# Kernel tables of a state-space mixer fetched as triangles, two channel groups interleaved

## What is computed

```
x, z = split(W_in @ hidden)
x = silu(conv4(x) + conv_b)
k = 2 * real(sum over n of Ct[h,n] * exp(dtA[h,n] * t)),  t = 0..511
y = causal_convolution(x, k) + x * D
y = y * silu(z);  out = W_out @ y
x1 = layernorm(hidden + out)
result = layernorm(x1 + expert_of(x1))      # 8 experts 128 -> 512 -> 128, the best one per token
```

## Time and profile before

| what | us |
|---|---|
| median of 3 executions | 283.48 (282.91 to 284.63) |
| the profiled execution, its own time | 282.02 |
| its span in the profile | 280.3 |
| projection until PE's last x product | 0 to 81.6 |
| group loop, PE | 83.8 to 131.6 |
| rest | 131.6 to 280.3 |

### The profile page before, as it was taken

How to read it: one execution, slowest core, us unless ns; L and a number is a source line. 1 busy time by engine, 2 the same in 40 slices (tenths; PEclk the granted TensorE clock), 3 DMA queues, 4 the chain that set the end, 5 groups by cost and what they waited for, 6 DMA issues and landing times.

```text
span 280.3 us, 8864 instructions
## 1 busy us (share of the span) xinstructions
PE 246.5 (88%) x2759; PEld 219.7 (78%) x2760; DVE 180.0 (64%) x585; ACT 177.2 (63%) x496; POOL 116.2 (41%) x175
## 2 busy tenths in 40 slices
PE   7999999999989799998988797375999999997970
PEld 4688888888878678776988696265989999897970
DVE  2689995997237688885445357720787666564772
ACT  4959999645997476764547061504667777675650
POOL 5000000400027576772254655573046565654555
PEclk9999999999999999999999959866899999999997
DMA  6619877549607999994933102713657666676500
GB/s 213 255 60 372 289 293 281 202 146 288 204 9 224 265 286 312 324 306 104 363 124 114 51 29 61 215 59 99 176 165 197 194 181 186 190 203 184 169 32 5
DMA packets 53627, 52.07 MB, mean 186 GB/s; under 512 B 4543, under 2 KB 42945, under 8 KB 53218
## 3 DMA queue, kind: packets, MB, share of 16 engines
q1 hardware_dynamic: 50866, 46.66, 54.8%
q0 software_dynamic: 2304, 4.34, 4.4%
q10 hardware_dynamic: 432, 0.79, 0.9%
HBM read 38.17 MB, written 14.05 MB: 186 GB/s over the span
## 4 chain that ended last, share of the span: by engine, by line
PE 72%; issue 8%; DVE 5%; another core or an unknown queue 4%; ACT 4%; DMA 4%; POOL 1%; SPq 1%; ACTq 0%; DVEq 0%; POOLq 0%
PE banks L1306 20%; PE banks L1510 9%; PE banks L1500 9%; PE banks L1384 6%; PE banks L1289 5%; PE banks L1455 4%; PE banks L1398 4%; PE banks L1394 3%; PE banks L1371 3%; PE banks L1446 2%; PE banks L1432 2%; ACT RE L770 2%; PE banks L1331 1%; DMA out<-X 1%
## 5 line engine op out<-in xcount | busy, mean ns | idle before, releaser
L807 ACT ACTIVATE Z<-banks,BR 128x128 f32<-128x128 f32 x156 | 44.7, 371 | 26.5 <-PE banks L1500 18.2
L1306 PE MATMUL banks<-Wx,XT 128*128 128x256 f32 x256 | 60.4, 382 | 0.0
L1306 PEld LDWEIGHTS banks<-Wx,XT 128*128 128x128 f32 x256 | 49.2, 192 | 7.0 <-issue 0.2
L576 POOL DMA_INDIRECT out<-X x39 | 38.4, 985 | 30.1 <-DVE X L1247 14.7
L1500 PE MATMUL banks<-Z 128*128 128x128 f32 x312 | 44.7, 289 | 6.0 <-ACT Z L796 4.2
L516 POOL TENSOR_TENSOR Wx<-BR,RE 128x384 f32 (+1 forms) x32 | 31.8, 1015 | 40.6 <-PE banks L1306 27.1
L1500 PEld LDWEIGHTS banks<-Z 128*128 128x128 f32 x312 | 40.8, 204 | 7.0 <-ACT Z L796 4.4
L1510 PE MATMUL banks<-BR,Z 128*128 x312 | 42.1, 279 | 0.7 <-DVE X L1230 0.7
L568 POOL DMA_INDIRECT dispatched_rows<-TR,CR x32 | 30.7, 960 | 25.9 <-DVE CR L1155 16.7
L1510 PEld LDWEIGHTS banks<-BR,Z 128*128 128x128 f32 x312 | 38.8, 196 | 1.1 <-issue 1.1
L1230 DVE TENSOR_TENSOR X<-banks,X 128x128 f32<-128x128 f32 x39 | 11.3, 289 | 22.5 <-PE banks L1510 15.8
(11 more groups left out here) (220 smaller groups left out, 455.5 us busy)
## 6 DMA issues: line engine op xcount, KB each, us to landing
TR<-kernel_rows SPq DMA_DIRECT2D x32, 512.0 KB, 6.3
Z<-w SPq DMA_DIRECT2D x39, 256.0 KB
dispatched_rows<-TR SPq DMA_DIRECT2D x3, 2310.0 KB, 9.0
X<-dispatched_rows SPq DMA_DIRECT2D x39, 66.0 KB
XT<-hidden_t SPq DMA_DIRECT2D x10, 256.0 KB, 4.2
RE<-decay_and_turns SPq DMA_DIRECT2D x2, 1024.0 KB, 5.2
BR<-w SPq DMA_DIRECT2D x1, 2048.0 KB, 8.1
dispatched_rows<-TR SPq DMA_DIRECT2D x1, 1848.0 KB, 7.9
```

The lines of the kernel that those rows point to most:

```text
L576: pool.indirect_dma_start(out_rows, bass.IndirectOffsetOnAxis(XS[:, n % ROWS_RING, TOKEN_COL:TOKEN_COL + 1].bitcast(U32), 0), F[:, slot, : ...
L807: last = nc.scalar.activation(HT[:, j, c * P:c * P + P], bank[UP_BANKS[j]][:, c * P:c * P + P], ACT.Relu, bias=B1[:, bass.ds(experts[j] * ...
L1306: last = mm(bank[X_BANKS[k]][:, j * CHAN:(j + 1) * CHAN], XT[:, slot, at:at + CHUNK], Wx[:, tap, :], start=(tap == 0), stop=(tap == TAPS - 1))
```

## The change

A pair of groups now shares one table tile. Two groups' kernel rows are interleaved sample by sample (`Kx` and `kernel_rows` have the pair index innermost), a ring slot holds a pair (4 slots of twice the size), and two transfers fill it: partitions 0 to 63 get 256 interleaved numbers per channel (1024 bytes in a run), partitions 64 to 127 get only the first 128 (512 bytes in a run). The rest of the lower half, the corner, is zeroed once per slot by Pool. PE reads the moving operand with a step of two elements and waits once per pair. The selectors, the order of groups in the kernel-row sums and the layout of `d_skip` follow. Besides, SP loads `cw_row` first, then `prm`, `row_params`, `cbias`; ACT runs a first Exp on one number, then the exponentials of `prm`, then those of `row_params`, and DVE follows that order.

```diff
-T_SLOTS = 8
+T_SLOTS = 4
+HALF = P // 2
...
-    kext = nc.dram_tensor("kernel_rows", [CHAN, KROW], F32).ap()
+    kext = nc.dram_tensor("kernel_rows", [P, KROW, 2], F32).ap()
-    toeplitz = bass.AP(kext.tensor, 0, [[1, P], [KROW, CHAN], [1, CHUNK]])
+    upper_rows = bass.AP(kext.tensor, 0, [[2, HALF], [KROW * 2, P], [1, 2 * CHUNK]])
+    lower_rows = bass.AP(kext.tensor, 2 * HALF, [[2, HALF], [KROW * 2, P], [1, 2 * HALF]])
...
-        TR = sb("TR", [P, T_SLOTS * GH * CHUNK])
+        TR = sb("TR", [P, T_SLOTS * GH * 2 * CHUNK])
...
+        Tpairs = TR[:, :].rearrange("p (s h u j) -> p s h u j", s=T_SLOTS, h=GH, j=2)
...
-            sp.dma_start(row_params, state_rows).then_inc(s_rparams, 16)
-            sp.dma_start(prm[:, :, :], states).then_inc(s_params, 16)
             sp.dma_start(cw_row[:, :], conv_w.rearrange("t c -> (t c)").unsqueeze(0)).then_inc(s_cw, 16)
+            sp.dma_start(prm[:, :, :], states).then_inc(s_params, 16)
+            sp.dma_start(row_params, state_rows).then_inc(s_rparams, 16)
+            sp.dma_start(cbias[:, :], conv_b.to_broadcast([P, CHAN])).then_inc(s_cb, 16)
             for b in range(2, A_BATCH):
                 load_batch(sp, b)
-            sp.dma_start(cbias[:, :], conv_b.to_broadcast([P, CHAN])).then_inc(s_cb, 16)
...
-            def load_toeplitz(r, k):
-                group = r * T_SLOTS + k
+            def load_toeplitz(r, m):
+                pair = r * T_SLOTS + m
                 if not isinstance(r, int):
-                    sp.wait_ge(s_tm, group - (T_SLOTS - 1))
-                sp.dma_start(Tring[:, k, :, :], toeplitz[:, bass.ds(group * GH, GH), :]).then_inc(s_t[k], 16)
+                    sp.wait_ge(s_tm, pair * 2 - (T_SLOTS - 1) * 2)
+                channels = bass.ds(pair * GH, GH)
+                sp.dma_start(Tring[0:HALF, m, :, :], upper_rows[:, channels, :]).then_inc(s_t[m], 16)
+                sp.dma_start(Tring[HALF:, m, :, 0:CHUNK], lower_rows[:, channels, :]).then_inc(s_t[m], 16)
...
+            def zero_corner(m):
+                nc.gpsimd.memset(Tring[HALF:, m, :, CHUNK:], 0.0).then_inc(s_tz, 1)
+            pool.wait_ge(s_const, 3)
+            zero_corner(1)
+            zero_corner(3)
+            pool.wait_ge(s_tz, 2)
...
-            nc.gpsimd.iota(brow, ...)
+            nc.gpsimd.iota(brow, ...).then_inc(s_pstep, 1)
+            pool.wait_ge(s_pstep, 6)
+            pool.wait_ge(s_kp, 1)
+            pool.wait_ge(s_fill, 16 * len(FILLS))
+            zero_corner(0)
+            pool.wait_ge(s_kd, 16)
+            zero_corner(2)
+            pool.wait_ge(s_tz, T_SLOTS)
             pool.wait_ge(s_a, PAIRS)
...
-            act.wait_ge(s_rparams, 16)
-            nc.scalar.activation(row_params[:, 0:2, :], row_params[:, 0:2, :], ACT.Exp).then_inc(s_rexp, 1)
+            act.wait_ge(s_v, LEAD)
+            nc.scalar.activation(ssq[:, 0, 0:1], rs[:, 0, 0:1], ACT.Exp)
             act.wait_ge(s_params, 16)
             nc.scalar.activation(sm[:, DT, :], prm[:, LOG_DT, :], ACT.Exp).then_inc(s_yt, LEAD)
             nc.scalar.activation(sm[:, EA, :], prm[:, LOG_A, :], ACT.Exp).then_inc(s_exp1, 1)
+            act.wait_ge(s_rparams, 16)
+            nc.scalar.activation(row_params[:, 0:2, :], row_params[:, 0:2, :], ACT.Exp).then_inc(s_rexp, 1)
...
-            tt(at, v(AMP)..., mask16..., ALU.mult).then_inc(s_sel, 1)
+            for j in range(2):
+                tt(at, amplitudes[:, :, :, j]..., mask16..., ALU.mult).then_inc(s_sel, 1)
...
-            nc.vector.tensor_copy(Kx[:, :, 0:CHUNK], backwards(KERNEL_BANK, CHUNK - 1, 2)).then_inc(s_kx, 2)
+            nc.vector.tensor_copy(Kx[:, 0:CHUNK, :].rearrange("p c j -> p j c"), backwards(KERNEL_BANK, CHUNK - 1, 2)).then_inc(s_kx, 2)
...
-                pe.wait_ge(s_t[k], (r + 1) * 16)
+                if k % 2 == 0:
+                    pe.wait_ge(s_t[k // 2], (r + 1) * 32)
...
-                    last = mm(yt[part:part + TILES, at:at + P], xg[:, h, :], Tring[:, k, h, :], start=True, stop=True)
+                    last = mm(yt[part:part + TILES, at:at + P], xg[:, h, :], Tpairs[:, k // 2, h, :, k % 2], start=True, stop=True)
...
             pe.wait_ge(s_const, 3)
+            pe.wait_ge(s_tz, T_SLOTS)
             pe.wait_ge(s_ctr, 1)
```

More of the change, by code:

```diff
@@ L291, in build @@
         s_t = [sem(f"toeplitz_loaded{k}") for k in range(T_SLOTS)]
+        s_tz = sem("toeplitz_zeroed")
         s_bc = sem("group_tables_ready")
@@ L415, in _ @@
             sp.wait_ge(s_kx, 3)
-            sp.dma_start(kext.rearrange("(j p) c -> p j c", p=P), Kx[:, :, :]).then_inc(s_kd, 16)
+            sp.dma_start(kext, Kx[:, :, :]).then_inc(s_kd, 16)
             sp.wait_ge(s_kd, 16)
             sp.wait_ge(s_fill, 16 * len(FILLS))
-            def load_toeplitz(r, k):
-                group = r * T_SLOTS + k
+            def load_toeplitz(r, m):
+                pair = r * T_SLOTS + m
                 if not isinstance(r, int):
-                    sp.wait_ge(s_tm, group - (T_SLOTS - 1))
-                sp.dma_start(Tring[:, k, :, :], toeplitz[:, bass.ds(group * GH, GH), :]).then_inc(s_t[k], 16)
-            for k in range(T_SLOTS):
-                load_toeplitz(0, k)
+                    sp.wait_ge(s_tm, pair * 2 - (T_SLOTS - 1) * 2)
+                channels = bass.ds(pair * GH, GH)
+                sp.dma_start(Tring[0:HALF, m, :, :], upper_rows[:, channels, :]).then_inc(s_t[m], 16)
+                sp.dma_start(Tring[HALF:, m, :, 0:CHUNK], lower_rows[:, channels, :]).then_inc(s_t[m], 16)
+            for m in range(T_SLOTS):
+                load_toeplitz(0, m)
             sp.wait_ge(s_xb, PAIRS)
             sp.dma_start(w_out_d, w_out).then_inc(s_wo, 16)
-            with sp.Fori(1, GROUPS // T_SLOTS) as r:
-                for k in range(T_SLOTS):
-                    load_toeplitz(r, k)
+            with sp.Fori(1, GROUPS // (2 * T_SLOTS)) as r:
+                for m in range(T_SLOTS):
+                    load_toeplitz(r, m)
             sp.wait_ge(s_y, GROUPS)
@@ L855, in _ @@
             nc.vector.memset(rs[:, 1, :], 1.0).then_inc(s_yc, LEAD)
-            dve.wait_ge(s_rexp, 1)
-            for i, factor, by in ((0, -1.0, 1), (1, TURN, 2)):
-                stt(row_rates[:, i, :], row_params[:, 0, :], factor, row_params[:, by, :], ALU.mult, ALU.mult).then_inc(s_rdec, 1)
             dve.wait_ge(s_exp1, 1)
@@ L864, in _ @@
             nc.vector.tensor_copy(v(TURNS), v(AI)).then_inc(s_dec, 1)
+            dve.wait_ge(s_rexp, 1)
+            for i, factor, by in ((0, -1.0, 1), (1, TURN, 2)):
+                stt(row_rates[:, i, :], row_params[:, 0, :], factor, row_params[:, by, :], ALU.mult, ALU.mult).then_inc(s_rdec, 1)
             done(ts(smt[:, 1, :], v(AI), 0.5, None, ALU.mult))
@@ L1344, in _ @@
             pe.wait_ge(s_xb, 8)
-            pe.wait_ge(s_sel, 1)
+            pe.wait_ge(s_sel, 2)
             pe.wait_ge(s_c, 2)
-            for half in range(2):
+            for j in range(2):
                 for q in range(4):
                     for strip in range(4):
-                        g = half * 16 + strip * 4 + q
-                        last = mm(bank[KERNEL_BANK][strip * 32:strip * 32 + 32, half * CHUNK:(half + 1) * CHUNK], Sel[:, g, :],
+                        g = strip * 8 + q * 2 + j
+                        last = mm(bank[KERNEL_BANK][strip * 32:strip * 32 + 32, j * CHUNK:(j + 1) * CHUNK], Sel[:, g, :],
                                   Ctab[:, g, 0:CHUNK], start=(q == 0), stop=(q == 3))
@@ L1407, in _ @@
             mm(bank[2][:, 0:EXPERTS], centre[:, 0:DM], gwT[:, :], start=True, stop=True).then_inc(s_gwp, 1)
-            with pe.Fori(0, GROUPS // T_SLOTS) as r:
-                for pair in range(0, T_SLOTS, 2):
+            with pe.Fori(0, GROUPS // (2 * T_SLOTS)) as r:
+                for pair in range(0, 2 * T_SLOTS, 2):
                     for k in (pair, pair + 1):
```

28 lines of the change are left out of this document (16 added, 12 removed).

## The result

| | median us | runs |
|---|---|---|
| before, beside the changed kernel | 282.79 (277.56 to 288.08) | 20 |
| changed | 285.09 (281.82 to 287.22) | 20 |
| ratio | 1.0157 (1.011 to 1.0204) | |

The changed kernel is slower by 1.1 to 2.0%, where a gain of 2.1 us was forecast. The time lies inside the range given, on the side of the first rival. The profiled execution took 286.02 us with a span of 284.3, against 282.02 and 280.3. A second measurement, in a later call, gave 1.0076 (1.0036 to 1.0117), so the sign holds and the size is uncertain by about a per cent. A ratio compares only executions within 1.5% of the fastest of their kernel, while a median takes in all of them, so the two need not agree to the last tenth of a per cent.

A forecast was written before the change was run, and what follows sets the result against it. PE was taken to bound the kernel, with tables running out at the loop's end. Start -0.7 and holes -1.42 summed to -2.1 us, taking profiled 282.02 to 279.9, carried over to 281.4; range 279.4 to 287.0.

The forecast's parts named there:

- the first rival: Table transfers: 64 partitions allow only 211 GB/s, t = 3.73, PE stands 4.7 us; 286.1 us, chance 0.30.
- the tables' term: Group loop: a pair's transfers take 2.66 or 1.77 us, below PE's 2.71, so the ring stays full.
- t: Group loop: the time a pair's table transfers take, forecast at 2.66 us if bytes set the pace.
- The stall formula: Group loop: PE would stand 12 t - 40.0 us for the last pair's table, nothing below t = 3.33.
- Start, -0.7: Kernel start: conv weights land earlier, so the broadcast starts at 4.2 or 4.25 instead of 4.98, gaining 0.7 us.
- the second rival: Early start triggers more: clock rises 3 us earlier or first-turn hole shrinks; another 0.5 to 2.4 us, chance 0.10.
- Holes at the end, -1.42: Loop's end: the two holes ahead of table products, 0.44 and 0.98 us, go, gaining 1.42 us.
- First-turn hole, 0: First turn of the loop: the 1.46 us hole is untouched, taken as 0, bounds -0.5 to +1.46 of gain.
- Step of two, 0: Table products: moving operand's 8-byte step costs 0, at most 14.4 us if each number cost twice.
- Exponentials, kernel rows, corners, 0: Work before the loop: new exponential order, kernel-row writes and Pool's corner memsets are hidden and cost nothing.
- the cover of 2.71 us at DVE's product: Kernel start: DVE idles 2.71 us ahead of L874, hiding the exponentials' new order; without it 0.3 us cost.
- The rest after the loop: Stage behind the loop: a change of more than a microsecond there would show the prediction wrong.

The follow-up runs named there:

- the two halves: Changed kernel fetching each pair's full square (1.049 MB) in two transfers, cut between partitions 63 and 64: 298.93 us, ratio 1.0565.
- the measurement with ACT's queue: Changed kernel with lower-half refills issued from ACT's queue and ACT's pair loop written out: 268.53 us, ratio 1.0182.
- the three-transfer kernel: Changed kernel fetching each pair's full square in three transfers, to partitions 0 to 31, 32 to 95 and 96 to 127: 280.41 us, ratio 1.0645.
- the order alone: Kernel before with only the order of first loads, exponentials and rates changed: 282.29 us, ratio 0.9948; run again 282.80 us, ratio 0.9941.
- the one transfer: Changed kernel fetching each pair's full square (1.049 MB) in one transfer to 128 partitions, no corners: 282.54 us, ratio 0.9979.
- the cut by channel: Changed kernel fetching each pair's full square in two transfers, each to all 128 partitions with half the channels: 281.88 us, ratio 0.9902.
- the kernel without refills: Changed kernel loading no table after the first four pairs, which later pairs reuse: 261.34 us, ratio 0.9905.
- tables alone: Changed kernel with the old order of loads, exponentials and rates: 287.41 us, ratio 1.0149.
- changed again: Changed kernel, unedited, measured once more in a later call: 286.10 us, ratio 1.0076.
- cut by columns: Changed kernel with first 128 numbers per channel sent to 128 partitions, the other 128 to the upper 64: 286.97 us, ratio 1.0063.

## Why the prediction was wrong

The failing step is the tables' term, "If bytes set the pace, a pair takes 3.55 x 0.75 = 2.66 us; if runs do, 1.77". Both took over the rate of transfers to 128 partitions for transfers to 64. The runs show t = 3.64 in place of 2.66. The stall formula fits: with the refills' first issue at 85.0 and the start's 0.71 taken off, it is 12 t - 39.8, or 3.9 us at 3.64, against 1.42 before. That is +2.5, less 0.7 for the start, +1.8; measured +1.87. As t was read from the last landing itself, this checks only the rest of the formula. With the rate of the full queue, t = 3.51, it would give 2.3 us of standing and +0.2: the formula left out that PE's own first hole stops the refills, which is the difference between 3.51 and 3.64. These 3.9 us don't all stand as holes ahead of table products, because PE loses time of its own under their cover: 2.52 us in the turn of the first hole (1.26 of it the hole, the rest the 1.2 GHz level behind it), 0.4 by the step of two, and 0.85 in the two holes, 3.8 in sum.

The first rival was right in its mechanism and near in its size: 211 GB/s and t = 3.73 from the fastest row, against 216 and 3.64. It forecast 286.1; the changed kernel took 285.09 and 286.10. I gave it 0.30 because 296 GB/s over 128 partitions was far below 422, and concluded that short runs set the pace. That inference was wrong in form. The right reading of the earlier trace rows was that no row showed a transfer to 64 partitions at any rate, and that the argument "296 is under 422" bounds nothing for them. The three cheap signs were in the text already: a bound of 211 GB/s, a need of 0.786 MB per 2.71 us, which is 290, and a first stall at t = 3.33, which is 236 GB/s. A change whose full gain needs 236 GB/s per transfer, from a shape never seen above an estimated 211, deserved the larger chance.

The page "SBUF — State Buffer" of the Trainium skill, section "Door 1: The DMA port swizzle", had this right in kind: a transfer to 64 partitions gets about half. The 196 GB/s that the prediction took from it is the page's measurement for a transfer of 1 MiB, and the 4.0 us worked out from it was too long. The same table gives about 218 GB/s as the limit for long transfers to 64 partitions; t would be 3.6 us by this figure, as an estimate, and the full queue of the two halves agrees with it (219 to 223 GB/s). Its section "Can I just issue two DMAs to hit both halves?", by which two transfers to the two halves serialize with a gain of 6%, was also right, and the measurement with ACT's queue agrees (240 GB/s in the mean against 233). By its explanation through ports, partitions 32 to 95 reach all of them; the three-transfer kernel agrees before the loop (258 GB/s against 223) and not in it (216).

The other steps:

- **Start, -0.7.** Right: the broadcast at 4.19, the loop 0.71 earlier; the order alone gave ratios of 0.9948 and 0.9941. With the tables as they are the loop's end does not feel it. In the first profile TensorE's clock rose with the work, 0.12 us behind it. In the second one it rose earlier and the loop started at 81.86 instead of 83.12, so the second rival, which had 0.10, came true in part of the executions; how large a part isn't known.
- **Holes at the end, -1.42.** Wrong with t. They became 0.85 and moved to the even groups. They do go where t allows it, in the one transfer and in the cut by channel. They also went in the second profile of the order alone, whose first hole was longer: time that PE loses early is time in which the tables catch up, so the holes can't be added up as if each stood alone.
- **First-turn hole, 0.** The direction was left open between -0.5 and +1.46 of gain; it grew by 1.26. That the change made it grow is not shown: the order alone had 2.55 us with the tables as before. It depends on table traffic, as the kernel without refills shows (0.08 us). In kernels with 128-partition transfers alone it was 1.45 to 2.55 us, in those with smaller ones 2.00 to 3.27, which overlaps too much to price the shape. The slow stretch of TensorE behind it was not forecast; its price is the half speed of three microseconds of work.
- **Step of two, 0.** Mis-sized by 0.4 us: 278 ns a product instead of 275.
- **Exponentials, kernel rows, corners, 0.** Right in the first profile, by luck for the corners. Of the cover of 2.71 us at DVE's product 0.47 is left: the start took 0.8 of it (the order alone has 1.93), and two DVE instructions that ran beside Pool's corners some 1.4, see below. Where the clock rose early the cover was gone, and the loop started at 81.86 and 81.80 with corners and at 80.98 without, so they cost 0.8 to 0.9 us by this comparison. That they could cost DVE anything was not forecast.
- **The rest after the loop.** From the loop's end to the span's end were 149.2 us before and 151.3 after, 2.1 more, as much as the loop itself lost, and more than the microsecond that the prediction named as a sign of being wrong. No instruction there was changed. Other profiles of the slower chips have 155.5 (order alone, an execution of 287.64 us), 152.7 (cut by channel), 152.5 (tables alone), 151.9 (changed again), 150.9 (order again), 150.9 (one transfer), 149.2 (two halves) and 148.6 (cut by columns), in no order that follows the tables. The loop alone, +1.87 of 280.3, would be 1.007, less than the interval of the first ratio. Whether the rest of 1.0157 comes from the change stays open.

## What to carry to other kernels

Fetch to all 128 partitions even if a quarter of the bytes is zeros: here 1.049 MB to 128 partitions took 2.72 us per pair at 385 GB/s, and 0.786 MB to two times 64 took 3.51 at 224. If a transfer must be cut, cut it along a free axis. And before a saving of bytes is counted, work out which rate it needs of the new shape, and look whether any row shows that shape at that rate.

## What was unexpected of the hardware

- **Half the partitions.** Transfers to one half of the partitions moved 219 to 223 GB/s in stretches with a full queue and 1024-byte runs, against 385 for 128 partitions with the same runs, in one transfer as in two cut by channel. The three transfers had 204 to 216 in the loop and 258 before it. The DMA engines count as fully busy in both (1.11 and 1.06 for the same bytes), so the share of the DMA engines does not tell a slow shape from a fast one; the GB/s beside it does.
- **Issues.** SyncE needs 0.60 us for an issue to 64 partitions with 512 runs (the changed kernel's median for the upper half) and 0.378 for one to 128 partitions with 512 runs (the cut by channel's). The one transfer, with 1024 runs to 128 partitions, has 0.373. The count of runs is not what it pays for.
- **Pool's memset and DVE.** Beside Pool's two memsets of the corners, two DVE instructions on 128 x 32 numbers took 0.82 and 0.89 us; their like took 0.18 a moment before. The same two instructions took 0.17 and 0.18 us in the order alone, which has no corners (5.20 and 5.41 us, second profile). Changed kernel, timeline:

```profile
4.72 0.18 DVE L883 COPY RE<-RE 128x32 f32<-128x32 f32 x1
...
5.14 1.87 POOL L516 MEMSET TR<- 64x1024 f32 x2
...
5.31 0.82 DVE L888 TENSOR_SCALAR RE<-RE 128x32 f32<-128x32 f32 x1
...
6.16 0.89 DVE L889 COPY RE<-RE 128x32 f32<-128x32 f32 x1
```

- **A hole that needs traffic.** 0.08 us without table refills, 1.45 to 3.27 with them, always in the first turn of PE's loop. Behind the holes of 2.53 us and more (the order alone among them) the granted clock of the stretch was below 1; so it was with the 2.00 us of the tables alone (0.81) and the 2.27 of the two halves (0.83), while with the 2.27 us of the one transfer, the 1.73 of the order alone and the 1.45 of the cut by channel it stayed at 1.00. So the length of the hole alone doesn't tell. The changed kernel's trace has one packet of an instruction queue from 92 to 96 us (0.02 MB), and the kernel without refills has one there too; that PE waits for such a packet, which shares the DMA engines with the tables, was not shown.
- **Chips.** The kernel before took 284.14 and 284.31 us on two chips and 264.69 on a third. From the loop's end to the end of the span the kernels on the third chip need 132.3 to 133.5 us, those on the others 148.6 to 155.5; that is most of the difference. Nothing here shows why.
